# Capsule routing: one round of tap sums per slot, with two product buffers for every tap

## What is computed

```python
patches = extract_patches(x, 3, 3, stride=(1, 1), pad=(1, 1))       # nine taps
priors = einsum('nfdhwij,ofijud->nhwofiju', patches, weight)         # 4 x 4 capsules of 8, per tap
logits = zeros_like(priors)
for r in range(3):
    probs = softmax(logits, axis=-3)
    out = sum(probs * priors, axis=-2, keepdims=True)
    if r != 2:
        out = squash(out)
        logits = logits + sum(priors * out, axis=-1, keepdims=True)
return squash(out)
# the network
x = x + capsules(group_norm(x))
x = x + attention_and_mlp_on_patches(group_norm(x))
```

## Time and profile before

| | |
|---|---|
| median of 3 runs | 12900.15 us (12896.17 to 12911.73) |
| the profiled execution | 12904.24 us |
| its span | 12902.4 us |
| TensorE busy | 12303.8 us (95%) |
| VectorE busy | 9188.1 us (71%) |
| ScalarE busy | 7592.3 us (59%) |
| GpSimd busy | 3414.9 us (26%) |

### The profile page before, as it was taken

One profiled execution on the slowest core, in us unless ns is written; L12 is line 12 of the kernel. 1 busy time (PEld: TensorE's weight loads), 2 busy tenths in 40 slices (PEclk: granted clock), 3 DMA queues, 4 the chain that ended last, 5 costly groups with the idle time before them and its releaser, 6 DMA issues. The chain is left out here.

```text
span 12902.4 us, 255523 instructions
## 1 busy us (share of the span) xinstructions
PE 12303.8 (95%) x73276; PEld 4675.7 (36%) x73276; DVE 9188.1 (71%) x17067; ACT 7592.3 (59%) x15286; POOL 3414.9 (26%) x3268
## 2 busy tenths in 40 slices
PE   6999999999993799999999999999999999999899
PEld 2333333333331233333333333333333333333233
DVE  6777777777776677777777777777777777777311
ACT  4666666666663366666666666666666666666411
POOL 4777777767772000000000000000000000000143
PEclk9999999999996799999999999999999999999999
DMA  3111111101104332232232232232232233232255
GB/s 78 22 20 18 22 19 19 22 17 21 22 15 131 74 72 67 68 73 67 67 74 67 66 75 67 66 75 67 65 75 68 65 74 69 65 73 68 68 122 111
DMA packets 853483, 772.61 MB, mean 60 GB/s; under 512 B 587092, under 2 KB 621492, under 8 KB 840884
## 3 DMA queue, kind: packets, MB, share of 16 engines
q1 hardware_dynamic: 850612, 747.43, 25.5%
q10 hardware_dynamic: 1536, 8.39, 0.3%
HBM read 510.63 MB, written 244.96 MB: 59 GB/s over the span
## 5 line engine op out<-in xcount | busy, mean ns | idle before, releaser
L1547 DVE TENSOR_REDUCE a_big<-a_mp 128x1 f32<-128x512 f32 x8192 | 5219.2, 684 | 1826.1 <-PE a_mp L1381 1807.4
L1467 ACT ACTIVATE a_ex<-a_sc 128x512 f32<-128x512 f32 x8192 | 4426.3, 601 | 1935.5 <-PE a_sc L1369 1930.6
L1381 PE MATMUL a_mp<-a_ks,a_qs 108*128 108x512 bf16 x8192 | 3131.1, 383 | 39.7 <-DMA a_ks<-qk_parts 24.9
L1369 PE MATMUL a_sc<-a_qs,a_ks 111*128 111x512 bf16 x8192 | 3124.5, 383 | 6.8 <-ACT a_ex L1467 4.5
L893 DVE TENSOR_TENSOR r_prod<-r_pg,r_win 128x512 f32<-128x512 f32 x2816 | 1846.1, 683 | 783.2 <-PE r_pg L618 438.6
L546 POOL TENSOR_TENSOR r_prod<-r_temp,r_win 128x512 f32<-128x512 f32 x1792 | 2095.8, 1189 | 1158.9 <-ACT r_temp L845 954.5
L1283 POOL TENSOR_TENSOR a_pieces<-a_left,a_pieces 128x512 bf16<-128x512 f32 x256 | 295.5, 1154 | 7323.9 <-ACT a_pieces L1453 7323.9
L1395 PE MATMUL a_po<-a_ex,a_va 128*32 128x512 f32 x16384 | 2182.0, 605 | 1.6 <-ACT a_oc L1473 0.9
L1369 PEld LDWEIGHTS a_sc<-a_qs,a_ks 111*128 111x128 bf16 x8192 | 794.9, 97 | 2477.4 <-ACT a_ex L1467 1767.8
L1381 PEld LDWEIGHTS a_mp<-a_ks,a_qs 108*128 108x128 bf16 x8192 | 803.1, 98 | 914.1 <-DVE a_big L1547 238.3
L845 ACT COPY r_temp<-r_pg 128x512 f32<-128x512 f32 x1792 | 975.3, 590 | 77.2 <-PE r_pg L618 38.6
(11 more groups left out here) (185 smaller groups left out, 11641.8 us busy)
## 6 DMA issues: line engine op xcount, KB each, us to landing
a_qs<-qk_parts SPq DMA_DIRECT2D x768, 144.0 KB
a_ks<-qk_parts SPq DMA_DIRECT2D x768, 144.0 KB
qk_parts<-a_pieces SPq DMA_DIRECT2D x128, 768.0 KB, 5.2
f_t<-mixed SPq DMA_DIRECT2D x48, 1536.0 KB, 16.6
a_tw<-second SPq DMA_DIRECT2D x512, 128.0 KB, 3.0
mixed<-a_t SPq DMA_DIRECT2D x256, 256.0 KB, 2.1
r_win<-first SPq DMA_DIRECT2D x128, 280.5 KB, 4.9
a_zw<-layered SPq DMA_DIRECT2D x192, 144.0 KB, 12.0
```

The source lines that it names most:

```text
L1369: pe.matmul(sc[k % BANKS][:, :], ks[0:KROWS + NPART, p.h, head, 128 * kb:128 * kb + 128], qs[0:KROWS + NPART, p.h, head, CHUNK * qb:CHUNK ...
L1381: pe.matmul(mp[k % BANKS][:, :], qs[0:KROWS, p.h, head, 128 * q:128 * q + 128], ks[0:KROWS, p.h, head, CHUNK * half:CHUNK * half + CHUNK], ...
L1467: nc.scalar.activation(ex[:, k % RING, :], sc[k % BANKS][:, :], ACT.Exp, scale=scale).then_inc(exped.sem, 1)
L1547: nc.vector.tensor_reduce(big[:, x % 2, k // 2:k // 2 + 1], mp[k % BANKS][:, :], AX_X, ALU.max).then_inc(maxed.sem, 1)
```

## The change

All three batches of slot s-1 are summed in one round in slot s, behind makes 0-3 and the first set of transposes. Batch 0 was summed at the end of its own slot. Every tap gets two product buffers, and both VectorE and GpSimd wait for the whole sum of slot s-2. `reduced` counts one per slot. The evacuations wait for the same moment as before, the end of batch 2. After the last pass the tail sums three batches rather than two.

```diff
-    prod = sb("prod", [128, TAPS, CHUNK])
-    prod_2 = sb("prod_2", [128, 2, len(POOLED), CHUNK])
+    prod = sb("prod", [128, 2, TAPS, CHUNK])
...
-    reduced = Signal(sem("reduced"), 3 * SLOTS, 1)
+    reduced = Signal(sem("reduced"), SLOTS, 1)
...
-        return prod_2[:, s % 2, POOLED.index(g), :] if g in pool_taps(s) else prod[:, g, :]
+        return prod[:, s % 2, g, :]
...
-            pool.wait_ge(reduced.sem, reduced.at(p.n, 3 * (s - 2) + batch_of[g] + 1))
+            pool.wait_ge(reduced.sem, reduced.at(p.n, s - 1))
...
-                last.then_inc(reduced.sem, 1)
                 return
...
-            last.then_inc(reduced.sem, 1)
+            if b == 2:
+                last.then_inc(reduced.sem, 1)
...
             if heavy and (s > 0 or -1 in which):
                 behind = p if s > 0 else p.to(-1)
-                batch(behind.n, (s - 1) % SLOTS, 1)
-                batch(behind.n, (s - 1) % SLOTS, 2)
+                for b in range(3):
+                    batch(behind.n, (s - 1) % SLOTS, b)
...
             for x in front[1:]:
                 light(p, x, which)
-            if heavy:
-                batch(p.n, s, 0)
...
-                act.wait_ge(reduced.sem, reduced.at(n, 3 * (8 * r + lane) + 3))
+                act.wait_ge(reduced.sem, reduced.at(n, 8 * r + lane + 1))
...
-            dve.wait_ge(reduced.sem, reduced.at(p.n, 3 * (s - 1) + batch_of[g] + 1))
+            dve.wait_ge(reduced.sem, reduced.at(p.n, s - 1))
             nc.vector.tensor_tensor(
-                prod[:, g, :].rearrange("p (a b) -> p a b", b=IMG),
+                product_at(s, g).rearrange("p (a b) -> p a b", b=IMG),
```

More of the change, by code:

```diff
@@ L414, in routing_phase @@
     pt = ctx.enter_context(nc.psum_tensor("r_pt", [128, CHUNK], F32))
-    batch_of = {g: b for b, gs in enumerate(BATCHES) for g in gs}
     fixed = sem("fixed")
@@ L650, in batch @@
                 pe.wait_ge(free.sem, free.at(n, k % LANES + 1 if k >= 0 else 1))
-            if BATCHES[b] == (8,):
+            if b == 1:
                 for q in range(BLK):
@@ L753, in slot @@
                 light(p, x, which)
-            if heavy:
-                batch(p.n, s, 0)
         def tail(p):
-            batch(p.to(-1).n, SLOTS - 1, 1)
-            batch(p.to(-1).n, SLOTS - 1, 2)
+            for b in range(3):
+                batch(p.to(-1).n, SLOTS - 1, b)
         run_slots(pe, passes, slot, tail)
@@ L775, in evacuate @@
             elif kind == "squash":
-                act.wait_ge(reduced.sem, reduced.at(n, 3 * (8 * r - 4 + lane) + 3))
+                act.wait_ge(reduced.sem, reduced.at(n, 8 * r - 4 + lane + 1))
                 nc.scalar.copy(sums[:, 1 + lane % 2, :], pl[:, :]).then_inc(sum_copied[r].sem, 1)
             else:
-                act.wait_ge(reduced.sem, reduced.at(n, 3 * (8 * r + lane) + 3))
+                act.wait_ge(reduced.sem, reduced.at(n, 8 * r + lane + 1))
                 nc.scalar.copy(logit[:, lane % 2, :], pl[:, :]).then_inc(logit_copied[r].sem, 1)
```

## The result

The change makes the kernel **slower: 12998.72 us** (median of 4 runs, 12994.42 to 13005.45) against 12900.46 (4 runs), a ratio of 1.0079 with an interval of 1.0066 to 1.0091, or +98 us. The forecast was 13041 with a range of 12850 to 13125. The experiments show that the +98 is the sum of two effects of opposite sign. One the prediction had at nearly its size, the other it had at nothing.

The account below looks back on a forecast made before the run. The fourth make's wait for VectorE's tap 7 product was taken to bound softmax slots, so the moved first sum is laid bare: 4.4 us a pass, 141 over 32 passes, 12900 + 141 = 13041 us, range 12850 to 13125.

Parts of the forecast that it names:

- the fourth make at 2086.16: Slot 5: it waits for VectorE's tap 7 product, TensorE arrives 0.75 us early, so the first sum's 0.99 cost nothing there.
- The order, by terms: Per-slot costs of moving the first sum behind makes 0-3: 4.4 us a pass, 141 us over 32 passes.
- 10, 11: Makes 4-7 of slot 10 come 0.6 us later, L717 of slot 11 1.0 later: +1.0 us a pass.
- four plain slots: Slots 4, 5, 12, 13: first sum's 0.87 less 0.28 of waiting for tap 8's product, +0.59 us each.
- Make 8 with makes 0-3 behind it: TensorE: make 8 followed directly by makes 0-3 should cost 0.96 us instead of 1.05.
- Slots 0-3: First sum adds 0.87 us in slot 0, slot 1 gives 0.24 back, L717 in slot 3 late: +1.6 a pass.
- Waits and buffers: Second product buffers, later sum waits and single count cost nothing; bounds 0.1 us a slot either way.
- Slot 6: Square L912, ending with GpSimd's L567, ends where it did, so slot 5's price falls to 0.03: -0.56 us a pass.
- Own work: Rival, chance 0.16: TensorE's own work decides, fewer changes of shape win 84 us: 12816, or 12720 with stalls filled.
- absorbed: Rival, chance 0.13: softmax slots' lag disappears in slots 6-9 and 13-15, effects cancel to within 26 us: 12900.
- worse: Rival, chance 0.09: the 0.87 is laid bare in nearly all slots, 8.3 us a pass, 265 us: 13165.
- The signs named beforehand: Profile after: fourth make apart near 1.7, L659 wait shrinks, makes 4-7 7.7 apart and unstretched, pass near 124.6 us.

Follow-up runs that it names:

- Experiment 6: VectorE's tap 7 product moved ahead of the light work in slots 2-5 and 10-13: on the changed kernel 12872.32 us, on the order-back kernel 12833.15 us.
- experiment 4: Order-back kernel with the first sum late only for slots 2-4 and 10-12: 12946.87 us; only for the other ten slots: 12881.71 us.
- experiment 5: Changed kernel with the matmuls of the first sum (taps 4, 5, 2, 3) left out, its waits kept: 12868.77 us.
- order back: Changed kernel with the first sum back in its old place behind make 8, two product buffers and single count kept: 12841.17 us; also called the order-back kernel.
- experiment 1: The run of the order-back kernel: changed kernel with the first sum in its old place, buffers and single count kept: 12841.17 us, ratio 0.9958 to before.
- experiment 2: Kernel before with one line moved, so VectorE's product waits first for the sum, then for the make; one buffer: 12846.55 us, ratio 0.9962.
- swapped kernel: The kernel of experiment 2: kernel before with VectorE's wait for the sum put ahead of its wait for the make: 12846.55 us.

## Why the prediction was right, and where it wasn't

**Direction and cause: right.** The decisive step was the fourth make at 2086.16: TensorE arrives too early and waits for tap 7's product, so what stands ahead of that make is free and what stands behind it is not. Experiment 6 takes the wait away and has 126 us back; experiment 4 puts only those six slots late and has 106 of the 157.5; experiment 5 finds the first sum nearly free in its old place.

**The order, by terms** (changed kernel less order back, medians of the table, us a pass):

```
slots        forecast   measured
0-3            +1.6       +1.1
4, 5           +1.18      +1.17
6              -0.56      +0.06   (against the kernel before: -0.61 where its clock stays)
7-9             0         -0.34
10, 11         +1.0       +1.1
12, 13         +1.18      +1.17
14, 15          0         +0.2
sum            +4.4       +4.5
```

The four plain slots were right to 0.01 us each; the first sum measured 0.88, with tap 8 behind it 0.22, for 0.87 and 0.24. Make 8 with makes 0-3 behind it took 2.00 us ahead of slot 1's sums (2108.97 to 2110.97), for the estimate of 2.03. Slots 0-3 came out lower because slot 0 lost 0.58 instead of 0.87. That slots 7 to 9 take something back was not foreseen, nor that 14 and 15 add some.

**Waits and buffers: wrong.** "I cost that wait at nothing, before and after" and "the counters cost nothing measurable" looked at when the semaphores are met, and they are indeed met early. It didn't ask how the wait is issued. Its form cost 0.09 us from make to product in the kernel before and, through the collision, 0.67 us more in slot 6, where the clock fell as well. The term was 0 and measured -54 us (experiment 1), -50 by the form alone (experiment 2). The bounds that the step gave, 0.1 us a slot either way or 51 us, hold the second and just miss the first.

**Slot 6: right in mechanism, wrong in account.** The -0.56 came from the collision of L912 with GpSimd's L567. Against the kernel before, slot 6 is 0.61 shorter where the clock stays (8.10 to 7.49), as if that were it. But the order-back kernel is 0.67 shorter there without any change of order. In the changed kernel the collision is there, milder:

```profile
2148.36 0.83 DVE L908 TENSOR_TENSOR r_sq<-r_cap 128x128 f32<-128x128 f32 x1
```
```profile
2147.84 1.21 POOL L565 TENSOR_TENSOR r_pr<-r_ex,r_rz 128x576 f32<-128x576 f32 x1
```

GpSimd's operation ends at 2149.05 and the square at 2149.19. From makes 4-7 of slot 4 the square starts 11.18 us later here and 10.60 in the order-back kernel, the 0.58 of slot 5's chain, so both explanations give slot 6 nearly the same number, and the comparison with the kernel before alone couldn't have told them apart.

**The rivals.** Own work (12816) and absorbed (12900) are out by the result, worse (13165) too. So they are by the order alone, 153 to 157 us where they had -84, 0 and 265. The signs named beforehand came: the fourth make 1.67 behind the first three's start, released by L889 (near 1.7 was said); the wait at L659 down to 54.3; 7.58 for 7.7 between makes 4-7; makes 4-7 of slot 2 an unstretched row of 1.14 us (at 2122.01); a pass of 124.3 for 124.6.

**The sum** (13041 for 12999) was 42 us too high: the order's term 16 too low, the missing term of the waits 54 too high (the rest is the 4 us by which the kernel before was faster in that comparison). It is partly luck that it came this near, since the two errors have opposite signs. The order's term also held slot 6's -0.56, 18 us a run, which belongs to the waits: without it, it was 159. The 4.5 us a pass of the table are 144 us of the order's 157.5; means instead of medians give 124.35 - 119.43 = 4.9. The falls of the clock, some 27 us of the changed kernel by my estimate and none in the order-back one, are in the means only. The prediction had no term for them; against the kernel before they nearly cancel, since it has 14 too.

## What to carry to other kernels

Work under a wait is free where it stands and costs its full length behind the wait: before moving a block to save changeovers, find the next instruction of that engine that waits for another engine's chain, and see on which side of it the block will lie. A merged row that is longer than its like (1.88 us for 1.14) can hold such a wait, easily overlooked at "95% busy"; look at the granted clock too, since a row at half clock is longer as well. When a change edits two things at once, undo one of them on the chip: here the half that looked harmless was the better one, and kept alone it gives 12841 us; with tap 7 moved in two slots and one sum late it gives 12811.

## What the runs showed of the hardware

- **A wait's threshold held in a register costs time when it changes.** With the wait for the data put on the register operation, VectorE's product began 0.085 us behind that operation and 1.29 us after the make's weight load; with the data's wait on the product itself, 1.20. This held in every one of 28 passes. In the loop the order of two waits in the source is worth 50 us of 12900, through what follows from it.
- **A hair decides a collision.** VectorE's square of two SBUF operands took 0.28 us when it began 0.04 us before GpSimd's operation, and 1.32 when it began 0.03 after. The Trainium skill ("SBUF — State Buffer", section "SBUF: two separate sides") says of the port that the two share that whichever starts first has it for the whole instruction. The trace agrees where GpSimd was first: the square ended 0.14 us behind it both times (2094.30 and 2149.19, against 2094.16 and 2149.05). Where GpSimd came second the trace agrees less clearly: its operation took 1.30 instead of 1.21, 0.09 more for an overlap of 0.24.
- **The clock falls behind some waits.** Between 400 and 3700 us of the kernel before, the clock was granted at half (1.2 GHz for 2.4) in 14 stretches, 48 us in all, and all 14 lie between the fifth makes of slots 5 and 6, where TensorE waits for tap 8. One of them, with the stretch before it:

```profile
1971.10:1974.50 3.40, 2.05 (x20) 0.64 (x18) 3.27 (x8) 1.54 (x4) 1.66 (x3) 1.00 0.00 0
1974.50:1977.91 3.41, 3.41 (x20) 1.23 (x12) 2.70 (x4) 1.69 (x3) 2.44 (x3) 0.50 0.00 0
```

  TensorE (first busy column) had 2.05 of 3.40 us of work before it fell. The order-back and the swapped kernel have no such stretch in that time. The changed kernel has 14 again, in slots 9, 12, 15 and 0 of the table; 8 of them lie in slot 12, which takes 9.27 with one and 7.58 without. There the fourth make waits for VectorE just before, though TensorE counts as busy for 3.28 of 3.41 us:

```profile
2067.05 0.29 PEld L620 LDWEIGHTS r_pg<-r_pr_t,r_widen 32*128 32x128 f32 x2 [0.95 <-DVE r_prod L889]
```
```profile
2064.87:2068.28 3.41, 3.28 (x16) 1.49 (x18) 3.41 (x9) 1.29 (x4) 2.59 (x3) 1.00 0.00 0
2068.28:2071.69 3.41, 3.41 (x24) 0.86 (x16) 1.24 (x3) 1.12 (x3) 2.62 (x3) 0.50 0.00 0
```

  The like wait in slots 4, 5 and 13 brings no fall, so which waits cost the clock stays open. Leaving out the first sum brought 58 falls: taking work away from TensorE cost it its clock, and by the estimate of experiment 5 all that it would have won on the order-back kernel.
- **Matmuls of two makes can interleave.** An fp32 make is two matmuls. In the changed kernel, make 8 of slot 3 (L616, one tile) and the makes of slot 4 (L620, all four tiles) come in this order:

```profile
2131.36 0.69 PE L616 MATMUL r_pg<-r_stack,r_wv 32*128 32x512 f32 x1
2131.55 0.69 PE L620 MATMUL r_pg<-r_pr_t,r_widen 32*128 32x512 f32 x1
2131.89 0.59 PE L616 MATMUL r_pg<-r_stack,r_wv 32*128 32x512 f32 x1
2132.08 2.50 PE L620 MATMUL r_pg<-r_pr_t,r_widen 32*128 32x512 f32 x7
```

  A make of the next slot starts between the two halves of make 8. It is likely why the two blocks together cost 2.00 us and not 1.05 + 1.07 = 2.12; which tile that matmul ran in the rows don't show.
